# Adding the attention mask on VectorE instead of by a matmul, and normalising x2 ahead of it in VectorE's order

## The chip, the cores and the metric

The program runs on one core of a Trainium2 chip. The metric is the device time of one execution in microseconds (us). Five engines work on their own instruction streams and meet only at semaphores: TensorE (PE in the profile, PEld for its weight loads), VectorE (DVE), ScalarE (ACT), GpSimd (POOL) and SyncE (SP). ACT and SP also issue the transfers (ACTq, SPq in the trace are the sequencers of these engines).

## The reference

128 items (B), each a 128 x 512 float32 matrix `x` (128 positions, 512 features), pass through four residual stages. The ids of an item choose its mask, adapter and category weights.

```
# stage 0: attention with a mask that depends on the item's kind (0, 1 or 2)
scores = einsum(tanh(x @ W1 + b1), v)                       # one score per position
mask   = prefix (l <= j), postfix (l >= j) or cloze (l != j)
p      = softmax(where(mask, scores, -1e30))                # rows j, columns l
x      = x + (p @ x) / cnt
# stage 1: adapter of the item's language, then layer norm, gamma, beta
h      = relu(x @ w1[lang] + b1) @ w2[lang] + b2
x      = x + norm(x + h) * gamma[lang] + beta[lang]
# stage 2: x = x + zX * lap_x(x) + zY * lap_y(x) + zR * x * (1 - x)
# stage 3: x = x + x @ W[cat] + b[cat]
```

## The kernel before, in words

Everything is unrolled in Python. An item is one tile of 128 partitions. The work is a software pipeline in slots: slot `s` does the attention of item `s`, the adapter of item `s-1`, the normalisation of item `s-2`, the stencil of item `s-3`, the transpose of `x3` for item `s-4` and the category matmul of item `s-5`. There are 133 slots; the first five fill the pipeline and the last five drain it. Items are sorted by category, and the 1 MB category weights `w3s` are loaded only when the category is a new one (otherwise the transfer is skipped).

No scheduler is involved: the order of every engine is the order in which its `slot` function calls the helpers, and each helper waits for the semaphores of what it reads and overwrites. An instruction that waits holds up everything behind it on its engine.

The names that matter here, with their lines in the profile:

- `attn_tanh` (L553, ACT) makes `attn`; `attn_scores` (L371 and L372, PE) multiplies a matrix `v_wide`, whose columns are all `v`, with `attn`, which puts the same score row on all 128 partitions of `ps_scores`, and then accumulates the mask by a second matmul, bfloat16 identity times mask.
- `row_max` (L694, DVE) takes the negated maximum of each row of `ps_scores`; `exponentials` (L503, ACT) makes `probs` and their sum; `denominator` (L715) and `row_scale` (L721) on DVE and `scale_rows` (L527, ACT) make `mix`; `mix_transpose` (L388, PE) and `add_identity` (L727, DVE) make `mixT`.
- `pool` (L400), `adapter_hidden` (L393), `adapter_project` (L382) and `adapter_up` (L409) are the PE's part of attention and adapter; `variance` (L518, ACT), `add_epsilon` (L744), `center` (L735) and `normalize` (L759, DVE) give `x2`.
- `add_columns` (L772) and `add_rows` (L782) on DVE give `x3`, which `x3_transpose` (L417, PE) turns, `move_x3T` (L497, ACT) copies and `category` (L431, PE) multiplies with the category weights.
- `load_params` (L239) reads an item's ids from SBUF into registers of one engine. In the instruction stream it is a `TENSOR_LOAD`. ACT reads three values with one such instruction per item, right after `scale_rows` and ahead of the transfer of the next `xT` (L569) and of `attn_tanh`; SP reads four; DVE reads one (the language), between `add_adapted` (L701) and `mean` (L707).

On ACT a slot runs: read the ids, issue the `xT` load (L569), `attn_tanh`, `variance`, issue the `x` load, `relu`, `column_ends`, `exponentials`, `reaction` (L543), `move_x3T`, `move_xw` (L511), issue the `b3` load (L576), `scale_rows`.

Of the kernel before, what the change touches and what calls it, by code (L numbers as in the profile page):

```python
# [12 lines left out]
P = 128  # L13
# [51 lines left out]
def cond_residual_kernel(nc, x, xT, ids, cols, w1a,  # L65
# [22 lines left out]
    with ctx:  # L88
# [3 lines left out]
        v_wide = sb("v_wide", [P, P])  # L92
# [6 lines left out]
        ident16 = sb("ident16", [P, P], BF16)  # L99
# [39 lines left out]
        attn = sb("attn", [P, 2, S])  # L139
        neg_max = sb("neg_max", [P, 2])  # L140
# [37 lines left out]
        def out_bank(j):  # L178
# [27 lines left out]
        score_tables, item_tables = sem("score_tables"), sem("item_tables")  # L206
# [14 lines left out]
        max_ready, denom_ready, scale_ready, mix_ready, x1_b2_ready, x1_beta_ready = (  # L221
            sem(n) for n in ("max_ready", "denom_ready", "scale_ready", "mix_ready", "x1_b2_ready", "x1_beta_ready"))
# [77 lines left out]
        def _(pe):  # L300
# [63 lines left out]
            def attn_scores(b, kind):  # L364
                pe.wait_ge(attn_ready, b.upto())
                if b.is_first:
                    pe.wait_ge(score_tables, 1)
                    pe.wait_ge(gconst, 3)
                if b.is_at_least(1):
                    pe.wait_ge(mixT_ready, b.upto(1))  # L370
                pe.matmul(ps_scores, v_wide[:, :], attn[:, b.ring(2), :], start=True, stop=False)  # L371
                pe.matmul(ps_scores, ident16[:, :], masks16[:, bass.ds(kind * P, P)], start=False, stop=True  # L372
                          ).then_inc(scores_mm, 1)
# [64 lines left out]
            def slot(s):  # L438
                if s.inside(B):
                    words[(s).n] = load_params(pe, LANG, 2, s)  # L440
# [14 lines left out]
                if s.inside(B):  # L455
                    attn_scores(s, words[(s).n][1])
# [15 lines left out]
        def _(act):  # L472
# [26 lines left out]
            def exponentials(b):  # L499
# [3 lines left out]
                nc.scalar.activation(probs[:, b.ring(2), :], ps_scores, ACT.Exp,  # L503
# [121 lines left out]
        def _(dve):  # L625
# [46 lines left out]
            nc.vector.tensor_scalar(v_wide[:, :], ident[:, :], 0.0, vals[:, V:V + 1], ALU.mult, ALU.add)  # L672
            nc.vector.tensor_copy(ident16[:, :], ident[:, :]).then_inc(score_tables, 1)
# [14 lines left out]

            def row_max(b):
                p = b.ring(2)  # L690
                dve.wait_ge(scores_mm, b.upto())
                if b.is_at_least(2):
                    dve.wait_ge(probs_ready, b.upto(2))
                nc.vector.tensor_reduce(neg_max[:, p:p + 1], ps_scores, AX.X, ALU.max, negate=True  # L694
# [105 lines left out]
            def slot(s):  # L800
                if s.inside(B):
                    row_max(s)
                if (s - 2).inside(B):
                    normalize(s - 2)
# [160 lines left out]
```

## Time and profile before

| | |
|---|---|
| median of 3 runs | 1071.29 us (1068.22 to 1071.43) |
| profiled execution, its own time | 1066.62 us |
| its span | 1064.8 us |
| PE busy | 1046.7 us (98%) |
| DVE busy | 890.6 us (84%) |
| ACT busy | 501.5 us (47%) |
| POOL busy | 528.0 us (50%) |
| TensorE's granted clock | full in all 40 slices |
| mean of the transfers | 252 GB/s |

The span runs from the first to the last recorded instruction; the rest of the execution's own time lies around it. In the groups of instructions `L694 DVE ... x128 | 36.2, 283 | 3.1` is the line, the engine, the count, the busy time in us, the mean duration in ns, and the idle time of the engine just before these instructions, with what ended it. A float32 matmul appears as two MATMUL records (two passes); their ends are modelled, so the distance between two starts tells what a pass costs. In the timeline the first column is the start and the second the duration, both in us, and "xN" counts instructions merged into one row.

### The profile page before, as it was taken

Reading aid. Unit: us, or ns where it says so; the run is one execution under the profiler, and the core shown is the slowest. Engines: PE = TensorE matmul, PEld = TensorE weight load, DVE = VectorE, ACT = ScalarE, POOL = GpSimd, SP = SyncE. Lnnn points to the kernel's source line nnn. Section 1 sums busy time; section 2 is a strip of 40 time slices with the busy share of each in tenths; the row PEclk is TensorE's granted clock in tenths of the full one; section 3 lists DMA queues with packets and bytes.
Section 4 is the critical chain, followed back from the end, with each engine's and each line's share of the span. In section 5 each row is a group of like instructions: output and inputs, shape, how many; then the busy total and the mean of one; then the engine's idle time right before and its main releaser. Section 6 shows DMA issues by size and latency. Waiting matters only on the chain.

```text
span 1064.8 us, 22722 instructions
## 1 busy us (share of the span) xinstructions
PE 1046.7 (98%) x4912; PEld 653.1 (61%) x4912; DVE 890.6 (84%) x2090; ACT 501.5 (47%) x1422; POOL 528.0 (50%) x537
## 2 busy tenths in 40 slices
PE   5999999999999999999999999999999999999998
PEld 3666666666666666666666666666666666666663
DVE  5788888888888888888888888888888988888886
ACT  3544544444444445445445444444444444444442
POOL 3355455455445545545545544554544554554454
PEclk9999999999999999999999999999999999999999
DMA  8787897687878987766786778788788788887875
GB/s 334 228 271 225 265 303 238 211 259 246 263 244 279 322 250 243 242 220 211 241 255 213 247 225 269 250 289 266 228 271 269 245 250 266 276 283 233 274 221 175
DMA packets 119108, 268.82 MB, mean 252 GB/s; under 512 B 13010, under 2 KB 13028, under 8 KB 111556
## 3 DMA queue, kind: packets, MB, share of 16 engines
q1 hardware_dynamic: 63428, 166.24, 47.8%
q10 hardware_dynamic: 55552, 101.15, 31.3%
q8 instruction: 48, 0.79, 0.3%
q14 instruction: 80, 0.66, 0.2%
HBM read 243.21 MB, written 33.55 MB: 260 GB/s over the span
## 4 chain that ended last, share of the span: by engine, by line
PE 96%; DVE 1%; issue 1%; DMA 1%; POOL 1%; ACTq 0%; ACT 0%; POOLq 0%; DVEq 0%; SPq 0%
PE ps_out L431 40%; PE bank_hidden L382 11%; PE ps_attn L360 11%; PE ps_adapt L409 10%; PE ps_pool L400 10%; PE ps_x3T L417 5%; PE bank_scores L371 3%; PE bank_hidden L393 3%; PE bank_scores L388 1%; PE bank_scores L372 1%; DMA b_wide<-in_b 0%; DMA col_rows<-in_cols 0%; POOL b_wide L909 0%; DVE ps_adapt L701 0%; POOL rows_near L902 0%
## 5 line engine op out<-in xcount | busy, mean ns | idle before, releaser
L431 PE MATMUL ps_out<-w3s,x3T 128*128 x1016 | 498.3, 600 | 0.8 <-ACT x3T L497 0.8
L896 POOL TENSOR_TENSOR neighbours<-x 128x510 f32<-128x510 f32 x128 | 132.6, 1036 | 214.9 <-DVE x L759 214.9
L431 PEld LDWEIGHTS ps_out<-w3s,x3T 128*128 128x128 f32 x1016 | 164.1, 191 | 103.1 <-issue 101.5
L888 POOL TENSOR_TENSOR rstd<-var_eps,minus_half 128x1 f32<-128x1 f32 x128 | 70.2, 548 | 272.1 <-DVE var_eps L744 272.0
L902 POOL TENSOR_TENSOR rows_near<-rows_near 128x512 f32<-128x512 f32 x128 | 162.8, 1272 | 30.5 <-DMA rows_near<-x 30.3
L360 PEld LDWEIGHTS ps_attn<-xts,w_attn 128*128 128x128 f32 x1024 | 134.3, 191 | 61.2 <-issue 60.9
L909 POOL TENSOR_TENSOR b_wide<-b_wide,x 128x512 f32<-128x512 f32 x128 | 162.7, 1271 | 4.2 <-DMA b_wide<-in_b 4.2
L553 ACT ACTIVATE attn<-ps_attn,vals 128x128 f32<-128x128 f32 x128 | 47.0, 367 | 246.6 <-issue 160.2
L360 PE MATMUL ps_attn<-xts,w_attn 128*128 128x128 f32 x1024 | 135.1, 275 | 0.5 <-issue 0.5
L382 PE MATMUL bank_hidden<-w_all,xts 128*128 x1024 | 135.4, 275 | 0.0
L701 DVE SCALAR_TENSOR_TENSOR ps_adapt<-ps_adapt,x_b 128x512 f32<-128x512 f32 x128 | 89.1, 696 | 52.3 <-PE ps_adapt L409 51.3
L409 PE MATMUL ps_adapt<-w_all,hid 128*128 x256 | 131.3, 594 | 0.0
L400 PE MATMUL ps_pool<-xs,mixT 128*128 128x512 f32 x256 | 130.9, 593 | 0.0
L382 PEld LDWEIGHTS bank_hidden<-w_all,xts 128*128 128x128 f32 x1024 | 124.6, 192 | 1.8 <-issue 1.7
L417 PEld LDWEIGHTS ps_x3T<-ident,x 128*128 128x128 f32 x512 | 62.6, 141 | 71.9 <-issue 45.8
L543 ACT ACTIVATE ps_react<-x,c_t,nzr_t 128x512 f32<-128x512 f32 x128 | 99.0, 774 | 3.8 <-DVE x L782 3.8
L735 DVE SCALAR_TENSOR_TENSOR ps_adapt<-ps_adapt,neg_mean,gamma_wide 128x512 f32<-128x512 f32 x128 | 96.9, 757 | 2.2 <-issue 0.8
L782 DVE SCALAR_TENSOR_TENSOR x<-rows_near,wide_rows,ps_react 128x512 f32<-128x512 f32 x128 | 94.5, 738 | 1.5 <-POOL rows_near L902 1.4
L772 DVE SCALAR_TENSOR_TENSOR ps_react<-neighbours,wide_rows,ps_react 128x512 f32<-128x512 f32 x128 | 95.5, 746 | 0.1
L759 DVE SCALAR_TENSOR_TENSOR x<-ps_adapt,rstd,x_beta 128x512 f32<-128x512 f32 x128 | 94.8, 741 | 0.8 <-POOL rstd L888 0.8
L497 ACT ACTIVATE x3T<-ps_x3T 128x512 f32<-128x512 f32 x128 | 75.7, 592 | 40.6 <-PE ps_x3T L417 40.2
L534 ACT ACTIVATE hid<-bank_hidden,vals 128x128 f32<-128x128 f32 x128 | 47.0, 367 | 98.0 <-PE bank_hidden L393 96.5
(114 smaller groups left out, 1326.9 us busy)
## 6 DMA issues: line engine op xcount, KB each, us to landing
w3s<-in_w SPq DMA_DIRECT2D x128, 1024.0 KB
rows_near<-x SPq DMA_DIRECT2D x256, 252.0 KB
xts<-in_xT ACTq DMA_DIRECT2D x128, 256.0 KB, 4.4
xs<-in_x ACTq DMA_DIRECT2D x128, 256.0 KB, 4.7
b_wide<-in_b ACTq DMA_DIRECT2D x128, 256.0 KB, 4.6
out_x<-res SPq DMA_DIRECT2D x128, 256.0 KB, 4.4
w_all<-in_w1l SPq DMA_DIRECT2D x1, 2560.0 KB, 10.9
w_all<-in_w2l SPq DMA_DIRECT2D x1, 2560.0 KB, 16.6
```

The lines of the kernel that those rows point to most:

```text
L360: mm = pe.matmul(ps_attn, w1_attn[:, k * A:(k + 1) * A], xts[:, r, k, :], start=(k == 0), stop=(k == K - 1))
L382: mm = pe.matmul(ps_xw, xts[:, s.ring(3), k, :], w1_all[:, bass.ds(lang * (K * A) + k * A, A)], start=(k == 0), stop=(k == K - 1))
L400: pe.matmul(ps_pool[:, :], mixT[:, d.ring(2), :], xs[:, d.ring(2), :], start=True, stop=True).then_inc(pool_mm, 1)
L409: pe.matmul(ps_adapt[:, :], hid[:, g.ring(2), :], w2_all[:, bass.ds(lang * D, D)], start=True, stop=True).then_inc(adapt_mm, 1)
L417: mm = pe.transpose(ps_x3T[:, k * P:(k + 1) * P], x3[:, i.ring(2), k * P:(k + 1) * P], ident[:, :])
L431: mm = pe.matmul(out_bank(j)[:, :], x3T[:, j.ring(2), k * P:(k + 1) * P], w3s[:, bass.ds(wslot * (K * D) + k * D, D)], start=(k == 0), sto ...
L543: nc.scalar.activation(ps_react[:, :], x2[:, h.ring(2), :], ACT.Identity, bias=c0_t[:, bass.ds(h.n, 1)], scale=nzr_t[:, bass.ds(h.n, 1)]). ...
L735: nc.vector.scalar_tensor_tensor(normed[:, :], y[:, :], neg_mean[:, q:q + 1], gamma_wide[:, bass.ds(lang * D, D)], ALU.add, ALU.mult).then ...
L772: nc.vector.scalar_tensor_tensor(ps_react[:, :], neighbours[:, q, :], zx_t[:, bass.ds(i.n, 1)], ps_react[:, :], ALU.mult, ALU.add).then_in ...
L896: nc.gpsimd.tensor_tensor(neighbours[:, q, 1:D - 1], x2[:, q, 0:D - 2], x2[:, q, 2:D], ALU.add).then_inc(neighbours_ready, 1)
L902: nc.gpsimd.tensor_tensor(above[:, q, :], above[:, q, :], below[:, q, :], ALU.add).then_inc(rows_ready, 1)
L909: nc.gpsimd.tensor_tensor(b3_wide[:, q, :], b3_wide[:, q, :], x3[:, q, :], ALU.add).then_inc(x3_b3_ready, 1)
```

## The change

The mask no longer goes through TensorE. `attn_scores` is one matmul whose weights are the column `v` broadcast over 128 columns (no `v_wide`, no `ident16`), and TensorE reads one id per item instead of two. A new VectorE helper `add_mask` adds the bfloat16 mask to `ps_scores` on the way out of PSUM into a new SBUF tile `masked`; `row_max` and `exponentials` read `masked`. VectorE therefore reads two ids per item (language and kind), one slot ahead. In VectorE's slot `normalize(s - 2)` now stands first, and `add_mask(s)` and `row_max(s)` behind it; before, `row_max(s)` stood first.

```diff
-            def attn_scores(b, kind):
+            def attn_scores(b):
                 pe.wait_ge(attn_ready, b.upto())
-                if b.is_first:
-                    pe.wait_ge(score_tables, 1)
-                    pe.wait_ge(gconst, 3)
                 if b.is_at_least(1):
                     pe.wait_ge(mixT_ready, b.upto(1))
-                pe.matmul(ps_scores, v_wide[:, :], attn[:, b.ring(2), :], start=True, stop=False)
-                pe.matmul(ps_scores, ident16[:, :], masks16[:, bass.ds(kind * P, P)], start=False, stop=True
-                          ).then_inc(scores_mm, 1)
+                pe.matmul(ps_scores, vals[:, V:V + 1].broadcast_to([A, P]), attn[:, b.ring(2), :],
+                          start=True, stop=True).then_inc(scores_mm, 1)
...
-                nc.scalar.activation(probs[:, b.ring(2), :], ps_scores, ACT.Exp,
+                nc.scalar.activation(probs[:, b.ring(2), :], masked[:, :], ACT.Exp,
...
+            def add_mask(b, kind):
+                dve.wait_ge(scores_mm, b.upto())
+                if b.is_first:
+                    dve.wait_ge(gconst, 3)
+                if b.is_at_least(1):
+                    dve.wait_ge(probs_ready, b.upto(1))
+                nc.vector.tensor_tensor(masked[:, :], ps_scores, masks16[:, bass.ds(kind * P, P)], ALU.add
+                                        ).then_inc(masked_ready, 1)
+
             def row_max(b):
                 p = b.ring(2)
-                dve.wait_ge(scores_mm, b.upto())
-                if b.is_at_least(2):
-                    dve.wait_ge(probs_ready, b.upto(2))
-                nc.vector.tensor_reduce(neg_max[:, p:p + 1], ps_scores, AX.X, ALU.max, negate=True
+                dve.wait_ge(masked_ready, b.upto())
+                nc.vector.tensor_reduce(neg_max[:, p:p + 1], masked[:, :], AX.X, ALU.max, negate=True
                                         ).then_inc(max_ready, 1)
...
             def slot(s):
-                if s.inside(B):
-                    row_max(s)
                 if (s - 2).inside(B):
                     normalize(s - 2)
+                if s.is_first:
+                    words[s.n] = load_params(dve, LANG, 2, s)
+                if s.inside(B):
+                    add_mask(s, words[s.n][1])
+                    row_max(s)
...
-                if s.inside(B):
-                    words[(s).n] = load_params(dve, LANG, 1, s)
+                if (s + 1).inside(B):
+                    words[(s + 1).n] = load_params(dve, LANG, 2, s + 1)
```

On DVE, the part of a slot of the full pipeline that follows `center`, before the change (L782 is `x3`, L694 the row maximum, L759 `x2`, L752 the result, L715 the denominator):

```order
L735 SCALAR_TENSOR_TENSOR ps_adapt<-ps_adapt,neg_mean,gamma_wide 128x512
L782 SCALAR_TENSOR_TENSOR x<-rows_near,wide_rows,ps_react 128x512 [waits x3T_mm,x3_b3_ready,rows_ready,columns_ready]
L694 TENSOR_REDUCE neg_max<-bank_scores 128x1 [waits probs_ready,scores_mm]
L759 SCALAR_TENSOR_TENSOR x<-ps_adapt,rstd,x_beta 128x512 [waits rstd_ready,norm_ready]
L752 TENSOR_TENSOR res<-ps_out,b_wide 128x512 [waits res_out1,x3_b3_ready,out_mm]
L715 TENSOR_SCALAR denom<-prob_sum,count_t 128x1 [waits probs_ready]
```

The same part after the change (L688 is the mask addition):

```order
L735 SCALAR_TENSOR_TENSOR ps_adapt<-ps_adapt,neg_mean,gamma_wide 128x512
L782 SCALAR_TENSOR_TENSOR x<-rows_near,wide_rows,ps_react 128x512 [waits x3T_mm,x3_b3_ready,rows_ready,columns_ready]
L759 SCALAR_TENSOR_TENSOR x<-ps_adapt,rstd,x_beta 128x512 [waits rstd_ready,norm_ready]
L688 ISA [waits probs_ready,scores_mm]
L688 TENSOR_TENSOR masked<-bank_scores,masks 128x128
L694 TENSOR_REDUCE neg_max<-masked 128x1 [waits masked_ready]
L752 TENSOR_TENSOR res<-ps_out,b_wide 128x512 [waits res_out0,x3_b3_ready,out_mm]
L715 TENSOR_SCALAR denom<-prob_sum,count_t 128x1 [waits probs_ready]
```

Between `x3` and the row maximum now stand `x2` and the mask addition; the result and the denominator follow as before.

On PE, the part of a slot around the scores, before the change (L388 turns `mix`, L393 is `adapter_hidden`, L400 `pool`):

```order
L388 MATMUL bank_scores<-ident,mix 128x128 [waits mix_ready]
L393 MATMUL bank_hidden<-mixT,xw 128x128 [waits mixT_ready,xw_ready]
L371 MATMUL bank_scores<-attn,v_wide 128x128 [waits mixT_ready,attn_ready]
L372 ISA
L372 MATMUL bank_scores<-masks,ident 128x128
L400 MATMUL ps_pool<-xs,mixT 128x512 [waits x1_beta_ready,x_in1]
```

The same part after the change:

```order
L383 MATMUL bank_scores<-ident,mix 128x128 [waits mix_ready]
L388 MATMUL bank_hidden<-mixT,xw 128x128 [waits mixT_ready,xw_ready]
L367 MATMUL bank_scores<-attn,vals 128x128 [waits mixT_ready,attn_ready]
L395 MATMUL ps_pool<-xs,mixT 128x512 [waits x1_beta_ready,x_in1]
```

One matmul and the register instruction ahead of it are gone, and the weights of the other one come from `vals`.

## Rows read from the trace of the kernel before

**Rows 1.** The page: busy time, share of the span and instructions; the chain that ended last.

```profile
PE 1046.7 (98%) x4912; PEld 653.1 (61%) x4912; DVE 890.6 (84%) x2090; ACT 501.5 (47%) x1422; POOL 528.0 (50%) x537
...
PE 96%; DVE 1%; issue 1%; DMA 1%; POOL 1%; ACTq 0%; ACT 0%; POOLq 0%; DVEq 0%; SPq 0%
```

**Rows 2.** Timeline of PE: the scores matmul of slots 6 and 127.

```profile
58.90 0.39 PE L371 MATMUL bank_scores<-attn,v_wide 128*128 128x128 f32 x2
...
1033.19 0.39 PE L371 MATMUL bank_scores<-attn,v_wide 128*128 128x128 f32 x2
```

**Rows 3.** Timeline of PE from the scores of slot 61 to the transpose of x3.

```profile
501.96 0.39 PE L371 MATMUL bank_scores<-attn,v_wide 128*128 128x128 f32 x2
...
502.19 0.22 PE L372 MATMUL bank_scores<-masks,ident 128*128 x1
...
502.24 1.08 PE L431 MATMUL ps_out<-w3s,x3T 128*128 x2
...
503.16 1.02 PE L400 MATMUL ps_pool<-xs,mixT 128*128 128x512 f32 x2
...
504.02 0.60 PE L417 MATMUL ps_x3T<-ident,x 128*128 128x128 f32 x4
```

**Rows 4.** Groups by line and shape: weight loads, the identity addition, the tanh.

```profile
L372 PEld LDWEIGHTS bank_scores<-masks,ident 128*128 128x128 bf16 x128 | 12.8, 100 | 0.0
...
L312 PEld LDWEIGHTS ps_pool<-lang_parts,pick 96*128 96x128 bf16 x5 | 0.5, 98 | 2.1 <-DVE beta_wide L686 2.1
...
L727 DVE TENSOR_TENSOR mixT<-bank_scores,ident 128x128 f32<-128x128 f32 x128 | 37.2, 290 | 25.1 <-PE bank_scores L388 23.3
...
L553 ACT ACTIVATE attn<-ps_attn,vals 128x128 f32<-128x128 f32 x128 | 47.0, 367 | 246.6 <-issue 160.2
```

**Rows 5.** Timeline of DVE in slot 50: x3, row maximum, x2, result.

```profile
414.69 0.74 DVE L782 SCALAR_TENSOR_TENSOR x<-rows_near,wide_rows,ps_react 128x512 f32<-128x512 f32 x1
415.34 0.29 DVE L694 TENSOR_REDUCE neg_max<-bank_scores 128x1 f32<-128x128 f32 x1
415.55 0.74 DVE L759 SCALAR_TENSOR_TENSOR x<-ps_adapt,rstd,x_beta 128x512 f32<-128x512 f32 x1
416.20 0.68 DVE L752 TENSOR_TENSOR res<-ps_out,b_wide 128x512 f32<-128x512 f32 x1
```

**Rows 6.** Timeline of PE in slot 50: the transpose of x3.

```profile
415.49 0.66 PE L417 MATMUL ps_x3T<-ident,x 128*128 128x128 f32 x4
```

**Rows 7.** Timeline of ACT and its sequencer, from the tanh of slot 50 to the next.

```profile
412.79 0.37 ACT L553 ACTIVATE attn<-ps_attn,vals 128x128 f32<-128x128 f32 x1 [2.94 <-issue]
...
415.67 0.37 ACT L503 ACTIVATE probs<-bank_scores,neg_max 128x128 f32<-128x128 f32 x1 [1.49 <-DVE neg_max L694]
...
417.71 0.40 ACT L527 ACTIVATE mix<-probs,scale 128x128 f32<-128x128 f32 x1 [0.23 <-DVE scale L721]
419.89 0.36 ACTq L569 DMA_DIRECT2D xts<-in_xT  x1
420.35 0.37 ACT L553 ACTIVATE attn<-ps_attn,vals 128x128 f32<-128x128 f32 x1 [2.24 <-issue]
```

**Rows 8.** Line 239 on ACT, then on DVE: duration ns min/median/max, first and last start.

```profile
L239 ACTq TENSOR_LOAD <-all_params x128: 705/1445/2673, 14.6 to 1013.3; - x128
...
L239 DVEq TENSOR_LOAD <-all_params x128: 307/696/1395, 25.2 to 1037.7; - x128
```

**Rows 9.** Timeline of slots 61 and 62: scaling, next xT issue, category weights.

```profile
506.14 0.40 ACT L527 ACTIVATE mix<-probs,scale 128x128 f32<-128x128 f32 x1 [0.32 <-issue]
...
507.71 0.34 ACTq L569 DMA_DIRECT2D xts<-in_xT  x1
...
512.11 0.36 SPq L263 DMA_DIRECT2D w3s<-in_w  x1
...
514.19 0.40 ACT L527 ACTIVATE mix<-probs,scale 128x128 f32<-128x128 f32 x1 [0.32 <-issue]
...
516.50 0.36 ACTq L569 DMA_DIRECT2D xts<-in_xT  x1
```

More of the change, by code:

```diff
@@ L91, in cond_residual_kernel @@
         w1_attn = sb("w1_attn", [P, K * A])
-        v_wide = sb("v_wide", [P, P])
         w1_all = sb("w1_all", [P, L * K * A])
@@ L98, in cond_residual_kernel @@
         ident = sb("ident", [P, P])
-        ident16 = sb("ident16", [P, P], BF16)
         masks16 = sb("masks16", [P, 3 * P], BF16)
@@ L139, in cond_residual_kernel @@
         attn = sb("attn", [P, 2, S])
+        masked = sb("masked", [P, S])
         neg_max = sb("neg_max", [P, 2])
@@ L205, in cond_residual_kernel @@
             sem(n) for n in ("b2_spread", "beta_spread", "b2_moved", "beta_moved"))
-        score_tables, item_tables = sem("score_tables"), sem("item_tables")
+        item_tables = sem("item_tables")
         params_made = sem("params_made")
@@ L219, in cond_residual_kernel @@
         edges_ready = sem("edges_ready")
-        max_ready, denom_ready, scale_ready, mix_ready, x1_b2_ready, x1_beta_ready = (
-            sem(n) for n in ("max_ready", "denom_ready", "scale_ready", "mix_ready", "x1_b2_ready", "x1_beta_ready"))
+        masked_ready, max_ready, denom_ready, scale_ready, mix_ready, x1_b2_ready, x1_beta_ready = (
+            sem(n) for n in ("masked_ready", "max_ready", "denom_ready", "scale_ready", "mix_ready", "x1_b2_ready", "x1_beta_ready"))
         y_ready, mean_ready, vareps_ready, norm_ready, x2_ready = (
@@ L439, in slot @@
                 if s.inside(B):
-                    words[(s).n] = load_params(pe, LANG, 2, s)
+                    words[(s).n] = load_params(pe, LANG, 1, s)
                     attn_project(s)
@@ L455, in slot @@
                 if s.inside(B):
-                    attn_scores(s, words[(s).n][1])
+                    attn_scores(s)
                 if (s - 5).inside(B):
@@ L671, in _ @@
             ins.then_inc(wide_made, 1)
-            nc.vector.tensor_scalar(v_wide[:, :], ident[:, :], 0.0, vals[:, V:V + 1], ALU.mult, ALU.add)
-            nc.vector.tensor_copy(ident16[:, :], ident[:, :]).then_inc(score_tables, 1)
             dve.wait_ge(sorted_made, 1)
```

## The prediction

> **What bounds the kernel now.** I read the page first, then PE's timeline, then the timelines of DVE and ACT in slots where they run late, and last the reads of ids into registers. The page says that PE is busy for 98% of the span and is 96% of the chain that ended last [rows 1]. The scores matmul starts at 58.90 in slot 6 and at 1033.19 in slot 127 [rows 2]: 121 slots in 974.29 us, 8.052 us each. So nearly everything depends on the length of a slot, and that of PE's instructions is what sets it, with next to no waiting.
>
> But a second chain runs beside PE, and it closes on itself once per slot. In slot 50 the tanh starts at 412.79 and the row maximum at 415.34 (2.55 later: variance on ACT, epsilon, center and x3 on DVE lie between and are all in a row), the exponentials at 415.67 (0.33), the scaling of the rows at 417.71 (2.04: reaction, the copies of x3T and xw), the next xT issue at 419.89 (2.18) and the next tanh at 420.35 (0.46) [rows 5, 7]. The reader should see in these rows that no link waits for PE: this is a ring through ACT, DVE and ACT again, of 5.38 us plus X, where X is the time from the scaling to the xT issue. X is the read of three ids into registers: 705 ns at best, 1445 at the median, 2673 at worst [rows 8], plus some 0.2 around it. X is 1.57 in slot 61, where no category weights are moving, and 2.31 in slot 62, in which they were issued 2.08 before the scaling [rows 9]. Its mean follows from the tanh group: 246.6 us idle ahead of 128 tanh is 1.93 each, and since the scaling takes 0.40 and the issue-to-tanh step is 0.46, X is about 1.93 + 0.40 - 0.46 = 1.87 [rows 4, 7]. The ring thus takes 7.25 on average against PE's 8.04. It has 0.8 to spare and only touches PE in single slots: in slot 50, x3 ends at 415.43 and PE's transpose starts at 415.49 right behind it [rows 5, 6], 0.06 late.
>
> **What the change removes from PE.** Seen from its start, the mask matmul lasts 0.05 until the next one (502.19 to 502.24). I don't trust that: from 501.96 to 503.16 there are two float32 passes over 128 columns, the mask, and two passes over 512 columns, 1.20 in all; two 512-column passes cost 0.86 (503.16 to 504.02), two 128-column ones 0.23 (501.96 to 502.19) [rows 3]. The mask therefore costs 0.11, the 0.10 of a weight load [rows 4] that the short bfloat16 pass doesn't cover for the matmul behind it. PE's own slot falls to 7.93.
>
> The Trainium skill (TensorE: Matmul & The Clock Gate, section Back-to-back issue gap) gives an isolated warm matmul of N columns N/2.4 + 2.5 ns, 56 ns here; by that PE would get back 0.056 a slot, half of what the rows say, and the same page warns that it leaves the weight load out. The rows decide.
>
> The weights of the scores now come from a broadcast column. The nearest rows: a broadcast bfloat16 load 98 ns, a plain one 100 [rows 4]; I take nothing. If a float32 one were slower, its cover is the pass before it, and what stands out would be at most another 0.10 a slot, eating the gain. The second id that PE no longer reads and the register instruction cost nothing now, since PE's sequencer runs ahead of it. The two set-up instructions removed on DVE lie ahead of a wait for PE and save nothing.
>
> **What it adds to the ring.** The row maximum stood 0.65 behind x3. Now x2 stands there (0.65 from its start to the next one, 415.55 to 416.20), then the mask addition, then the maximum [rows 5]. The addition is a 128x128 read of PSUM and SBUF like the identity addition, 0.29 [rows 4]; the maximum must wait for its result, so nothing overlaps, and I add 0.04 for the semaphore. From x3 to the row maximum that is 0.65 + 0.65 + 0.33 instead of 0.65: 0.98 more. It is the largest term of the change, and no part of it is covered in a slot where the ring is late, because x3, x2, the mask and the maximum are consecutive on one engine and ACT waits for the maximum. The exponentials read SBUF now instead of PSUM: no row separates the two, between -0.03 and +0.03, taken as 0. From the exponentials to the scaling I take 1.93 instead of 2.04: the scaling in slot 50 waited for the reciprocal on DVE [rows 7], and that comes earlier behind the exponentials now, since x2 no longer stands between. The ring is 5.38 + 0.98 - 0.11 = 6.25 plus X.
>
> X itself: DVE now reads two ids, at the same time as ACT reads three. The bounds for what this does to X are 0 and one register's share, (705 - 307)/2 = 0.20 [rows 8]. Against that, the ring is later behind the issue of the category weights, so that less of their transfer is left when the ids are read; at best every X would be 1.57. X thus lies between 1.57 and 2.07, and I take 1.85. The ring is then 8.10.
>
> **The sum.** The ring at 8.10 is above PE's 7.93, so PE waits at the transpose of x3; queued behind that on PE are the adapter's projections, adapter_up and the next item's attention, and DVE and ACT wait for those. The slot goes from 8.05 to 8.10: 121 x 0.05 = +6 us, where PE alone would have given 121 x -0.12 = -14. Slow and quick X alternate, and a slot cannot be shorter than 7.93, so some of the quick ones are wasted; I add 0.01 a slot, +1. In the five slots of filling, PE has waits anyway and the longer chain counts between 0 and 0.98 a slot, 0 to +5; I take +2. In the drain the ring is gone after the last item, and DVE enters it up to 1 later; +1. Total +10: the profiled execution's 1066.6 becomes 1077, and the median of the runs, 4.7 above it, becomes 1071.3 + 10 = 1081.
>
> DVE's own load is no bound: 890.6 us busy and 128 x 0.33 = 42 more is 933 of some 1075 [rows 1]. A slower mean, because two ids are read ahead of it, comes 0.2 to 0.4 later; the variance waits for the tanh later than that.
>
> **The rivals.**
> 1. PE stays the bound. If X falls towards 1.57 because the category weights are out of the way, the ring is 7.82 and every slot 7.93 to 7.97: -14 to -10, plus 3 for fill and drain, 1061 to 1065. For it: slot 61 shows that X without that traffic is 1.57, and with the items sorted by category many slots load none. Against it: the mean of 1.87 is what 128 slots gave, and it would have to fall by 0.2. This is the case that is not slower, and it decides at a mean X of 7.93 - 6.25 = 1.68.
> 2. The ring is as long as PE's slot was. With X near 1.77 the slot is 8.02 to 8.04, fill and drain add 3, and the time is 1068 to 1074, no difference that can be measured.
> 3. The ring is worse than I say: no shortening behind the exponentials (+0.11), and X at 1.87 plus part of the register's share. The slot is 8.25 to 8.35, +24 to +36, plus 4: 1099 to 1111. For it: the mean X as it stands, with 2.04 and 0.98, already gives 8.23. Against it: the reciprocal does come earlier.
> 4. The change doesn't take the mask's 0.11 off PE, since the broadcast weights load slower or since the next weight load was never exposed. It would only move rival 1 to between 1066 and 1071 and leaves the forecast, which the ring sets, where it is.
>
> **How the numbers follow.** The forecast (ring binds, slot 8.05 to 8.20, 1074.5 to 1093) has 0.42, rival 3 0.17, rival 2 0.16 and rival 1 with the faster part of rival 4 0.25. A measurement of this kernel can tell 0.3%, 3.2 us, from no change. Slower by more than that is the forecast and rival 3, with a little of it lost at the border: 0.58; within it 0.17; faster 0.25. The time predicted is the forecast's, 1081. The range takes in most of rival 1 and the lower part of rival 3: 1062 to 1100; for the forecast alone it is 1074 to 1093.
>
> **What would show it.** The pass over the mask is gone and the two starts around it, scores to pool, are 1.09 apart instead of 1.20. Row maximum behind x3 by 1.63 instead of 0.65. The tanh of a typical slot starts less than 1 us ahead of the scores matmul, and PE shows waits for x3 at its transpose in most slots, not in a few. Slots of 8.0 to 8.2 with the ones that load weights the longest. The ring's account is wrong if PE still shows no waits and all slots are 7.93, and the size of X is wrong if the mean idle time ahead of the tanh is not between 1.5 and 2.1.

## The result and the profile after

The changed kernel takes 1066.20 us (median of 20 runs, 1062.28 to 1071.08), the kernel before 1069.58 in the same comparison (20 runs, 1068.11 to 1075.32). The ratio is 0.9965 with a 95% interval of 0.9952 to 0.9978: faster by 0.35%, little but clear of zero. The forecast was 1081, slower. The profiled executions lie closer together than the medians: 1065.58 after, with a span of 1063.7, against 1066.62. A trace shows one execution, and those of the changed kernel are spread over 9 us: counts of slots from two traces that differ by a few say little.

The page after, answering to [rows 1]: busy time per engine, then the chain that ended last.

```profile
PE 1040.2 (98%) x4784; PEld 639.1 (60%) x4784; DVE 918.9 (86%) x2216; ACT 480.7 (45%) x1422; POOL 528.2 (50%) x537
...
PE 40%; issue 32%; POOL 21%; DVE 2%; POOLq 0%; ACTq 0%; DVEq 0%; ACT 0%
```

PE has 128 instructions fewer and is 6.5 us less busy. And the chain has moved: it was PE for 96%, now PE is 40%, and the rest is put down to POOL (21%) and to "issue" (32%). That is not the ring of ACT and DVE: traced back, the chain stays on POOL there, through waits for which it names no cause. So this line says that PE is no longer all of it, and the timelines have to say what the rest is. That PE's share fell and the kernel did not get slower is the first thing to explain.

PE's timeline, answering to [rows 2, 3]: the scores matmul of slots 6 and 127, and in slot 59 from the scores over the pool matmul to the transpose of x3.

```profile
61.77 0.39 PE L367 MATMUL bank_scores<-attn,vals 128*128 128x128 f32 x2
...
489.17 0.39 PE L367 MATMUL bank_scores<-attn,vals 128*128 128x128 f32 x2
...
490.25 1.02 PE L395 MATMUL ps_pool<-xs,mixT 128*128 128x512 f32 x2
491.11 0.60 PE L412 MATMUL ps_x3T<-ident,x 128*128 128x128 f32 x4
...
1032.23 0.28 PE L367 MATMUL bank_scores<-attn,vals 128*128 128x128 f32 x1
```

The 121 slots take 970.46 us now against 974.29 [rows 2]. From scores to pool it is 1.08 instead of 1.20 [rows 3]. Taken slot by slot from the same matmul, a slot of the kernel before is nearly always 8.04 us: 7 slots are longer by over 0.03 and the excess of all is 1.1 us. In the changed kernel 91 slots are within 0.03 of 7.93, and 30 are longer, with 10.4 us over it in all. So the profiled execution sums up as: fill +2.9 (slot 6 begins at 61.77, not at 58.90), PE's own slots 121 x -0.109 = -13.2, long slots 10.4 - 1.1 = +9.3, drain -0.1: together about -1.0, which is what the two executions differ by.

Timeline of DVE in slot 59, answering to [rows 5]: x3, x2, mask, row maximum. Behind it the groups of the mask's addition, the exponentials and the tanh, by line, answering to [rows 4].

```profile
489.35 0.74 DVE L782 SCALAR_TENSOR_TENSOR x<-rows_near,wide_rows,ps_react 128x512 f32<-128x512 f32 x1
490.01 0.75 DVE L759 SCALAR_TENSOR_TENSOR x<-ps_adapt,rstd,x_beta 128x512 f32<-128x512 f32 x1
490.67 0.28 DVE L688 TENSOR_TENSOR masked<-bank_scores,masks 128x128 f32<-128x128 f32 x1
490.99 0.29 DVE L694 TENSOR_REDUCE neg_max<-masked 128x1 f32<-128x128 f32 x1
```

```profile
L688 DVE TENSOR_TENSOR masked<-bank_scores,masks 128x128 f32<-128x128 f32 x128 | 35.8, 280 | 3.0 <-PE bank_scores L367 3.0
...
L498 ACT ACTIVATE probs<-masked,neg_max 128x128 f32<-128x128 f32 x128 | 51.5, 402 | 216.0 <-DVE neg_max L694 215.9
...
L548 ACT ACTIVATE attn<-ps_attn,vals 128x128 f32<-128x128 f32 x128 | 47.0, 367 | 230.6 <-issue 159.5 <-PE ps_attn L359 71.1
```

The row maximum stands 1.64 behind x3, as forecast. The tanh group has 230.6 us of idle ahead of it, 1.80 each; by the forecast's own working X is 1.80 + 0.40 - 0.46 = 1.74, and counted over the 120 slots of the full pipeline that another xT issue follows it is 1.79 on the mean (forecast 1.85; before the change, counted in the same way, 1.93).

Now the ring, in the slot before. The timeline of ACT with its sequencer, and of SP for its first line: category weights issued, scaling, xT issue, tanh, and a turn later exponentials, scaling, xT issue and tanh (answers to [rows 7, 9]).

```profile
474.82 0.36 SPq L262 DMA_DIRECT2D w3s<-in_w  x1
```

```profile
477.26 0.40 ACT L522 ACTIVATE mix<-probs,scale 128x128 f32<-128x128 f32 x1 [0.21 <-issue]
479.97 0.34 ACTq L564 DMA_DIRECT2D xts<-in_xT  x1
480.42 0.37 ACT L548 ACTIVATE attn<-ps_attn,vals 128x128 f32<-128x128 f32 x1 [2.76 <-issue]
...
484.28 0.40 ACT L498 ACTIVATE probs<-masked,neg_max 128x128 f32<-128x128 f32 x1 [2.38 <-DVE neg_max L694]
...
485.00 0.34 ACTq L571 DMA_DIRECT2D b_wide<-in_b  x1
...
486.02 0.39 ACT L522 ACTIVATE mix<-probs,scale 128x128 f32<-128x128 f32 x1
487.01 0.34 ACTq L564 DMA_DIRECT2D xts<-in_xT  x1
487.45 0.37 ACT L548 ACTIVATE attn<-ps_attn,vals 128x128 f32<-128x128 f32 x1 [1.04 <-issue]
```

Timeline of PE at the scores matmul and of PEld at the transpose of x3 in the slot that the tanh at 480.42 leads to, and behind them the wait of that line over the whole run (us, times, longest), after and then before.

```profile
481.12 0.39 PE L367 MATMUL bank_scores<-attn,vals 128*128 128x128 f32 x2
...
483.11 0.42 PEld L412 LDWEIGHTS ps_x3T<-ident,x 128*128 128x128 f32 x4 [0.72 <-DVE x L782]
```

```profile
PEld ps_x3T L412 <- DVE x L782: 37.4, 56, 1.8
```

```profile
PEld ps_x3T L417 <- DVE x L782: 25.3, 53, 1.3
```

With weights issued 2.44 us ahead of the scaling, X is 2.71; the tanh comes 0.70 ahead of the scores matmul of its slot and not 1.8, x3 comes late, and PE's weight loads wait for it. Such a wait is not yet a long slot: the kernel before has 53 of them and 7 long slots. One turn later, with no weights moving, X is 0.99 and the lateness is made good. And from the exponentials at 484.28 to the scaling it is 1.74, not 1.93.

Counted over the same 121 slots, from the same starts: 53 slots have a weights transfer issued in the 4.5 us ahead of their scaling (an issue of 0.36 us; one that is skipped takes 0.11), 68 have none. X has two values, not one (the last slot with weights has no next xT issue, so that 52 count for its mean):

| slots | X before | X after | long slots after | excess, us |
|---|---|---|---|---|
| 68 without weights | 1.70 | 1.35 | 0 | 0.0 |
| 53 with weights | 2.23 | 2.36 | 30 | 10.4 |

The links of the ring without X are 0.45, 1.90, 1.63, 0.32 and 1.74: 6.04. The ring is 7.39 in the first class, well below PE's 7.93, and 8.40 in the second. (The expectation of experiment 12 has 2.31 for 2.36, since it counts the slot without a next xT issue as nothing.) All 30 long slots are of the second class, as the 7 of the kernel before were. But 53 x 0.47 would be 25 us, and the excess is 10.4: in slots that are not long the tanh starts 1.77 us ahead of the scores matmul (the median), in the long ones 0.42 to 0.90. A late turn first uses up that lead, and quick turns restore it.

### The profile page after: what moved, and what is told of

It reads as the page before. It is cut to its first block, busy times and chain, and to the rows that moved or that the text cites. A ratio compares the mean times of both kernels' runs of the same rounds, so it can differ in the third digit from the quotient of the medians.

```text
span 1063.7 us, 22593 instructions
## 1 busy us (share of the span) xinstructions
PE 1040.2 (98%) x4784; PEld 639.1 (60%) x4784; DVE 918.9 (86%) x2216; ACT 480.7 (45%) x1422; POOL 528.2 (50%) x537
## 4 chain that ended last, share of the span: by engine, by line
PE 40%; issue 32%; POOL 21%; DVE 2%; POOLq 0%; ACTq 0%; DVEq 0%; ACT 0%
PE ps_out L426 17%; POOL b_wide L912 8%; POOL rows_near L905 8%; PE bank_hidden L377 5%; PE ps_attn L359 4%; PE ps_adapt L404 4%; PE ps_pool L395 4%; POOL rstd L891 4%; PE ps_x3T L412 2%; POOL neighbours L899 2%; DVE x L759 1%; PE bank_hidden L388 1%; PE bank_scores L367 1%; PE bank_scores L383 1%; DVE x L782 1%
## 5 line engine op out<-in xcount | busy, mean ns | idle before, releaser
L426 PE MATMUL ps_out<-w3s,x3T 128*128 x1016 | 491.7, 593 | 0.8 <-ACT x3T L492 0.8
L426 PEld LDWEIGHTS ps_out<-w3s,x3T 128*128 128x128 f32 x1016 | 164.1, 191 | 101.6 <-issue 101.5
L548 ACT ACTIVATE attn<-ps_attn,vals 128x128 f32<-128x128 f32 x128 | 47.0, 367 | 230.6 <-issue 159.5
L498 ACT ACTIVATE probs<-masked,neg_max 128x128 f32<-128x128 f32 x128 | 51.5, 402 | 216.0 <-DVE neg_max L694 215.9
L759 DVE SCALAR_TENSOR_TENSOR x<-ps_adapt,rstd,x_beta 128x512 f32<-128x512 f32 x128 | 95.4, 745 | 1.1 <-POOL rstd L891 1.0
L782 DVE SCALAR_TENSOR_TENSOR x<-rows_near,wide_rows,ps_react 128x512 f32<-128x512 f32 x128 | 94.5, 738 | 1.5 <-POOL rows_near L905 1.4
L765 DVE TENSOR_TENSOR ps_react<-ps_react,x 128x512 f32<-128x512 f32 x128 | 88.2, 689 | 0.9 <-ACT ps_react L538 0.9
## 6 DMA issues: line engine op xcount, KB each, us to landing
w_all<-in_w1l SPq DMA_DIRECT2D x1, 2560.0 KB, 10.4
```

The lines of the kernel that those rows point to most:

```text
L426: mm = pe.matmul(out_bank(j)[:, :], x3T[:, j.ring(2), k * P:(k + 1) * P], w3s[:, bass.ds(wslot * (K * D) + k * D, D)], start=(k == 0), sto ...
L759: nc.vector.scalar_tensor_tensor(x2[:, q, :], normed[:, :], rstd[:, q:q + 1], x1_beta[:, q, :], ALU.mult, ALU.add).then_inc(x2_ready, 1)
L782: nc.vector.scalar_tensor_tensor(x3[:, q, :], above[:, q, :], zy_t[:, bass.ds(i.n, 1)], ps_react[:, :], ALU.mult, ALU.add).then_inc(x3_rea ...
```

## The experiments

Four questions: what the order and the addition cost alone, whether the ring decides the long slots, what makes X long, and which version is best. Each run was timed against the kernel before on the same chip; I give the ratio to that. X and slots are counted from each trace as above, X without the last slot.

**1. The mask's move alone, x2 behind the row maximum.** The changed kernel with

```diff
-                if (s - 2).inside(B):
-                    normalize(s - 2)
                 if s.is_first:
                     words[s.n] = load_params(dve, LANG, 2, s)
                 if s.inside(B):
                     add_mask(s, words[s.n][1])
                     row_max(s)
+                if (s - 2).inside(B):
+                    normalize(s - 2)
```

> The changed kernel with one thing put back: VectorE does the mask addition and the row maximum first and x2 behind them, as the order was before. Theory R (a slot lasts as long as the longer of PE's stream, 7.94 us, and the ring tanh, x3, x2, mask, row maximum, exponentials, scaling, ids, tanh): x2's 0.66 leaves the ring, which falls from 6.06 + X to 5.40 + X, about 7.2 with the mean X of 1.80. The 30 of 121 slots above 7.94 should shrink to a few, slot mean 7.94 to 7.96, and filling gets about 2 us shorter: 9 to 12 us under the changed kernel, 1054 to 1057. Rival P (PE alone sets the slot, and the long slots come from transfers or from PE's own issue): the same 1066 as the changed kernel, with about 30 long slots. Rival V (VectorE's total load counts): 1066 too, since its work is the same.

1069.07 us, ratio 0.9987 (0.9972 to 1.0002). The forecast was missed by over 12 us. Slot 6 begins at 58.88, so the 2.9 us of fill belong to x2 in front; but there are 45 long slots, with 14 us over 7.93. From x3 to the row maximum it is 0.97, 0.66 less. But from the exponentials to the scaling it is 2.05 in late slots and no longer 1.74, because the reciprocal now comes behind x2 (the scaling's waits for it are the last two rows below). So the fixed links are 5.69, only 0.35 shorter. X took the rest back in slots without weights: 1.94 instead of 1.35, with 18 long slots among them; with weights it is 2.27. Line 238 on ACT and the wait at the transpose in this kernel (duration ns min/median/max, first and last start; us, times, longest), then the scaling's wait for the reciprocal in this kernel and in the changed one:

```profile
L238 ACTq TENSOR_LOAD <-all_params x128: 702/1930/3099, 14.2 to 1013.2; - x128
```

```profile
PEld ps_x3T L412 <- DVE x L782: 49.5, 89, 1.2
```

```profile
ACT mix L522 <- DVE scale L721: 27.4, 94, 0.8
```

```profile
ACT mix L522 <- DVE scale L721: 1.1, 2, 0.8
```

The median read is 1930 ns, where the changed kernel has 1374. X is no constant that a ring can be built from: it depends on where in the slot it falls.

**2. The order alone.** The kernel before with normalize(s - 2) ahead of row_max(s), mask on PE.

> The kernel before with only the order changed: x2 ahead of the row maximum, mask still by matmul. Theory R: the ring grows by 0.66 less what the reciprocal gives back, to about 5.75 + X, 7.6 on average against PE's 8.04. More slots than the 7 of before touch it, but few: slot mean 8.055 to 8.09, 0 to +5 us, and filling up to +3: 1070 to 1077. Rival P: 1069.6, no change. If x2 first were a gain of its own (x2 and its transfers start 0.2 us earlier), it would be faster than 1069.6.

1074.53 us, ratio 1.0036 (1.0021 to 1.0050). Fill +2.3, and 28 long slots. From x3 to the row maximum it is 0.66 more, from the exponentials to the scaling 1.70 and not 2.04, so that the ring is 0.32 longer. x2 ahead of the maximum costs by itself; it is no gain that the mask's move hides.

**3. The mask left out.** The kernel before without the second matmul of the scores; start=True, stop=True on the first.

> The kernel before without the mask matmul and without any mask in its place: the mask is left out of the computation, the rest is as before. It prices PE's part alone. Theory R with 0.11 us for the mask matmul: slots of 7.94, ring 5.38 + X well below, so 121 x 0.11 = 13 us less, 1055 to 1058. Rival: the mask matmul is worth its own 0.05 as the distance of the starts says, 6 to 7 us less, 1062 to 1064, with slots of 7.99.

1061.98 us, ratio 0.9908 (0.9891 to 0.9926). The number is the rival's, but not its reason: the common slot is 7.93, so that the pass does cost PE its 0.11 (0.109). In the traced execution, the slowest of six at 1065.22, there are 44 long slots with 12.9 us in all, 38 of them with weights, and X is 2.64 in the slots with weights. Even without any addition on DVE, a quicker PE runs into the ring.

**4. A second addition.** The changed kernel with one more of the same additions, into a tile that nobody reads, ahead of the real one.

> The changed kernel with the mask addition done twice: the first into a spare tile that nobody reads, the second as before. It adds 0.21 to 0.28 us to the ring and nothing to PE. Theory R: ring 6.30 + X, about 8.1 on average, above PE's 7.94: well over half of the slots go long, slot mean 8.10 to 8.20, 10 to 22 us over the changed kernel, 1076 to 1088. Rival P: 1066. Rival V: VectorE rises from 86% to 89% busy, still idle at times: 1066 to 1067.

1079.58 us, ratio 1.0079 (1.0064 to 1.0095), within theory R's range. x3 to row maximum is 1.83, 0.20 more. 55 slots are long instead of 30 (theory R had well over half of the 121), 46 of them with weights, with 22.1 us in all: 11.7 more than in the changed kernel, and the fill takes another 3.4. 0.20 in each of 55 slots is 11.0, so the ring decides in about half of the slots, and there nearly in full.

**5. The ids read and the xT issue out of the ring.** ACT waits 1.7 us on the mean for the row maximum; from the second item on they now stand in that wait.

```diff
-                if (s + 1).inside(B):
+                if (s + 1).inside(B) and s.n < 1:
                     words[(s + 1).n] = load_params(act, CAT, 3, s + 1)
                     load_xT(s + 1, words[(s + 1).n][1])
...
                     column_ends(s - 4)
+                if (s + 1).inside(B) and s.n >= 1:
+                    words[(s + 1).n] = load_params(act, CAT, 3, s + 1)
+                    load_xT(s + 1, words[(s + 1).n][1])
                 if (s - 1).inside(B):
                     exponentials(s - 1)
```

> The changed kernel with one move: ScalarE reads the next item's three ids and issues its xT load in its wait ahead of the exponentials, not behind the scaling of the mix, so X is no part of the ring of VectorE and ScalarE. Theory R (the ring decides the 30 long slots): the ring is then 6.0 to 6.3 us, far below the tensor engine's 7.94, so the long slots' 9.7 us go but for those that weights or first items cause: 1055 to 1060 us, PE above 98%. Rival F (the long slots come from somewhere else, from the four neighbour rows and the DMA queues): 1063 to 1067 us, the count of long slots near 30 as in the changed kernel. Rival C (the ids read then stands in the wait and is itself slow, 1.4 to 2.9 us, so that it pushes the exponentials): over 1068 us, row maximum to exponentials longer than 0.4.

1056.79 us, ratio 0.9884 (0.9863 to 0.9905), as the ring has it. Seven slots are long, with 2.0 us. The chain, the wait at the transpose, and the read in this kernel:

```profile
PE 90%; issue 3%; DVE 2%; POOL 1%; DVEq 0%; ACT 0%; ACTq 0%; POOLq 0%
```

```profile
PEld ps_x3T L412 <- DVE x L785: 11.2, 29, 1.2
```

```profile
L238 ACTq TENSOR_LOAD <-all_params x128: 692/707/1335, 14.6 to 1008.2; - x128
```

PE is the chain again. What I had not foreseen is that the read itself is 707 ns at the median there, as fast as it ever is.

**6. SyncE reads its ids ahead of the neighbour rows.** load_params(sp, FRESH, 4, s) ahead of shift_rows(s).

> The changed kernel with one move: SyncE reads its four ids ahead of the three neighbour-row copies, so that its read no longer starts about when ScalarE's does. Theory S (X is long when ScalarE's ids read meets SyncE's read): X falls to 1.0 to 1.3 us in most slots, from a mean of 1.80, long slots fewer than 30, 1058 to 1063 us. Rival T (X is long because of the copies and loads on the DMA queues, not of the other engine's read): X stays 1.6 to 1.9 on the mean, 1064 to 1068 us. Rival U (SyncE's read, now ahead of the copies, delays them, and x3 and the reaction come late): 1068 us or more, with the tensor engine waiting for x3.

1067.89 us, ratio 0.9981 (0.9962 to 0.9999). X is 1.64 on the mean instead of 1.79, long slots are 24 with 10 us. ACT's read still has 1386 ns at the median, and in 120 of 121 slots SP's read is over by then. SyncE's read beside it is not what makes it long: theory S falls. The move is not without effect, though: X is 1.77 in the slots with weights instead of 2.36, and 1.54 in the others instead of 1.35. It also puts the rows' copies nearer to ACT's read.

**7. Without the category's weights.** SyncE loads them for the first two items only.

> The changed kernel without the category's weights after the first two items (all later items are computed with the first two items' weights): the 1 MB-class loads of SyncE are gone, everything else stands. Theory T (X is long because of the traffic of the weights): X falls from a mean of 1.80 to 1.0 to 1.3, 1056 to 1062 us. Theory S (X is long because of the other engines' reads): X 1.6 to 1.8 and 1063 to 1067 us.

1056.14 us, ratio 0.9876 (0.9853 to 0.9899). No slot is over 7.94. The ids read and the wait:

```profile
L238 ACTq TENSOR_LOAD <-all_params x128: 698/730/1967, 13.6 to 1006.6; - x128
```

```profile
PEld ps_x3T L412 <- DVE x L783: 5.2, 5, 1.8
```

X is 1.08. It is 1.09 in the slots that had no weights in the changed kernel either, where it was 1.35. One thing goes with it: without the weights SyncE issues the neighbour rows earlier, 2.77 us ahead of ACT's read at the median, where it was 2.23 in the changed kernel's slots without weights and 1.99 in those with. So the run does not tell the weights themselves from the place of the rows.

**8. VectorE reads its ids once.** It starts its own read 0.27 us behind ScalarE's in nearly every slot, so it was a suspect as well.

> The changed kernel with VectorE reading its two ids for the first item only (all later items take the first item's mask and language in VectorE's additions). Theory V (ScalarE's ids read is long because VectorE's starts 0.27 us behind it): X falls by 0.5 to 0.8 in the slots without weights and by 0.5 or more in those with, long slots under 15, 1056 to 1061 us. Theory Q (it is long because of the neighbour rows and the weights on the DMA queues and SyncE's read): X falls by under 0.3, 1062 to 1067 us, the long slots still those with weights.

1065.11 us, ratio 0.9947 (0.9928 to 0.9966). X is 1.34 and 2.39, long slots 31, all with weights.

```profile
L238 ACTq TENSOR_LOAD <-all_params x128: 697/1346/2820, 13.5 to 1011.2; - x128
```

ACT's read is what it was (1374 at the median): theory Q, not V.

**9. VectorE reads two ids in the kernel before.** The count in load_params(dve, LANG, ...) is 2 instead of 1.

> The kernel before with VectorE reading two ids instead of one (the second is not used). Theory R: VectorE's read grows by 0.2 us, the ring's X by 0.0 to 0.2, which the kernel before has room for: 1068 to 1071 us. Rival H (a longer read of VectorE slows the other engines' reads by as much as it is longer, 0.4 on the mean): X over 2.2, long slots 25 or more, 1072 to 1077 us.

1070.59 us, ratio 1.0010 (0.9993 to 1.0026), no difference. X is 1.93 on the mean in both. The second id costs nothing that the times can show; the one trace has 21 long slots with 3.3 us, against 7 with 1.1.

**10. The ids read out of the ring, in the kernel before.** The edit of experiment 5.

> The kernel before with one move: ScalarE reads the three ids and issues the xT load in its wait ahead of the exponentials; the mask stays on the tensor engine and x2 behind the row maximum. Theory R (ring and tensor engine by slot): the kernel before had 7 long slots with 1.45 us in all over its floor of 8.04, so that taking X out of its ring can give back 1 to 3 us at the most: 1065 to 1069 us; the 12 to 13 us that the move gave beside the mask's move are then the 0.105 us a slot of the mask matmul, which only the move lets through. Rival G (the ids read itself is worth its time everywhere, also where the tensor engine bounds): 1056 to 1062 us.

1066.09 us, ratio 0.9969 (0.9953 to 0.9985). Every slot is 8.04, none is long. Out of the ring the read is worth 0.3% where PE's slot is 8.04, and 9 to 12 us where it is 7.93 (experiments 5 and 11, against the changed kernel and experiment 1).

**11. Mask moved, x2 behind, ids in the wait.** Experiments 1 and 5 together.

> Both moves: the mask's addition by VectorE, x2 back behind the row maximum, and ScalarE's ids read and xT load in the wait ahead of the exponentials. Theory R: the ring is 5.4 us, the floor of the tensor engine 7.94 in nearly every slot, and the fill that putting x2 first cost is back (2.9 us): 1052 to 1057 us, 2 to 4 us below the kernel with the ids read in the wait and x2 first. Rival F (x2 behind the row maximum delays the neighbour rows, and the tensor engine waits at the transposes of x3): 1060 to 1068 us, long slots 20 or more.

1055.44 us, ratio 0.9874 (0.9851 to 0.9896): the lowest median of all kernels here (its interval overlaps that of experiment 5), 14 us below the kernel before in the same comparison, and by the two ratios 0.9% below the changed kernel. Ten slots are long, with 2.5 us; the fill is back (slot 6 begins at 59.07). ACT's wait is shorter here than the read and the issue in it: the exponentials start 0.92 behind the row maximum and not 0.32, which the ring has room for.

```profile
PE 94%; issue 2%; DVE 2%; POOL 1%; DMA 1%; DVEq 0%; ACT 0%; ACTq 0%; POOLq 0%; SPq 0%
```

**12. Weights issued behind the neighbour rows.** If weights ahead of the read are the trouble, they could go a little later.

```diff
                     shift_rows(s)
+                if (s - 1).inside(B):
+                    load_w3(s - 1, ...)
+                if s.inside(B):
                     words[(s).n] = load_params(sp, FRESH, 4, s)
...
-                if s.inside(B):
-                    load_w3(s, ...)
```

> The changed kernel with one move in SyncE's order: an item's category weights are issued behind the next item's three neighbour-row copies, not ahead of them, so that the weights no longer enter the queues 2.45 us before ScalarE's ids read. Theory W (in the changed kernel all 30 long slots are among the 53 with weights, where X is 2.31 on the mean against 1.35 without, because the weights lie ahead of the rows and of the read): X falls below 1.9 in nearly every slot, long slots under 10, 1056 to 1060 us. Rival N (the weights only move, and now lie under the read itself, or come late for the tensor engine): X 2.2 or more in the slots with weights, or a wait of the tensor engine for the weights, 1064 to 1072 us.

1073.15 us, ratio 1.0025 (1.0006 to 1.0044). Both were half right, and the time is above both ranges. X fell to 1.21 in the slots whose items bring weights and 1.24 in the others, and the wait for x3 nearly went. But PE now waits for the weights. ACT's read; then the waits of PEld for x3 and ahead of the category's weight loads (101.5 us in the changed kernel); then the worst place on PE's timeline:

```profile
L238 ACTq TENSOR_LOAD <-all_params x128: 700/884/2243, 14.4 to 1021.6; - x128
```

```profile
PEld ps_out L427 <- issue: 117.3, 413, 2.9
...
PEld ps_x3T L413 <- DVE x L783: 4.3, 7, 1.7
```

```profile
237.06 1.05 PE L360 MATMUL ps_attn<-xts,w_attn 128*128 128x128 f32 x8
240.27 1.46 PE L427 MATMUL ps_out<-w3s,x3T 128*128 x2 [2.16 <-issue]
```

The profile calls that wait "issue", since the landing of the weights has no instruction to be put down to; that it is the weights I infer from the edit and from the line. The 24 long slots have 15.8 us over 7.93. PE itself idles for 10.4 us in 12 such waits; part of the rest is the lower clock behind the longest of them (last section). The place of the weights is a trade between ACT's read and PE's own need.

## Why the prediction was wrong

**What bounds the kernel** was read rightly: PE, and beside it a ring of ACT and DVE that touches it in single slots. Experiments 4 and 5 show both: 0.20 more in the ring made nearly twice as many long slots, and cutting it made every slot but seven PE's own.

**The removal from PE** was right in size: 0.109 a slot in the changed kernel and in experiment 3, forecast 0.11. The Trainium skill (TensorE: Matmul & The Clock Gate, section Back-to-back issue gap) would have given 0.056 for an isolated pass of 128 columns, and about 0.081 in a stream of weight loads and matmuls; the measurement is above both and decides. The broadcast column costs nothing: 192 ns a load before (`v_wide`) and after (`vals`). Rival 4 falls.

**The addition to the ring** was right: x3 to row maximum 1.63 to 1.64 against 1.63 forecast, the mask's addition 280 ns against 290.

**The exponentials** I took at no cost for reading SBUF. They went from 368 to 402 ns, 0.03 more, the upper end of my bounds. The Trainium skill (Perfetto Trace Analysis, section Optimizing Scalar/DVE Operations) has an overhead of about 93 ns for ScalarE on SBUF and about 51 ns on PSUM, 42 ns apart; the trace has 34, the same way and near it.

**From the exponentials to the scaling** is the first step that failed: "From the exponentials to the scaling I take 1.93 instead of 2.04". It is 1.74 in slots that are late, in slot 58 too. I had let the reciprocal come earlier, but not followed ACT's queue behind that: with nothing to wait for it is 1.10 to the x3T copy, 0.48 to xw and 0.16 to the scaling, and the b3 issue at 485.00 runs under the reaction. The order of x2 is what does it: with the mask on PE, x2 first brings this link from 2.04 to 1.70 (experiment 2), and with x2 put back it is 2.05 (experiment 1). So x2 first adds 0.66 to the ring and takes 0.3 away, where I had taken away 0.11. The ring is 6.04 + X, not 6.25 + X, and by my own threshold, 7.93 less the ring, PE stays the bound up to a mean X of 1.89 and not 1.68. X is 1.79. That alone moves the case from the forecast to rival 1.

**X** is the second step. Its mean was forecast well (1.85, measured 1.79), partly by luck: I had it fall because less of the weights' transfer would be left, and in the slots with weights it rose, from 2.23 to 2.36, while it fell in those without, from 1.70 to 1.35. And "The ring is then 8.10" put it into every slot. X has two values, which [rows 9] showed in two neighbouring slots and which I noted in the reading and then averaged away. 68 slots are at 7.93 whatever the ring does below that, and the 53 with weights pay only what is above it, less the lead that the slots between give back. How much each step is worth can be estimated from the trace: I carry the tanh's lead from slot to slot with the measured X; a scaling is never earlier than 4.07 behind the scores matmul (slot 57), PE is late when the lead is under 0.81 (slot 58: 0.70, and 0.11 over 7.93), and a scores matmul never starts less than 0.42 behind its tanh. With links of 6.04 that gives 29 long slots and 10 us, as measured; with the forecast's 6.25 it gives 17 us, and with 6.04 and X at its mean in every slot none. The forecast had 121 x 0.17 = 21 us over PE's floor. So of the 10 us too many some 7 are the first step and 3 the mean; and once the links are right, the mean would hide the 10 us that are there. That and the fill were to be set against 13.

**The fill** cost 2.9, forecast 2, within its bounds of 0 to 5; it comes from x2 ahead of the maximum (2.3 with that alone in experiment 2, nothing without it in 1 and 11). The drain cost nothing, forecast 1.

**Rival 1**, PE stays the bound, is nearest with 1061 to 1065; the median is 1.2 above it. It too is not quite what happened, since it had "every slot 7.93 to 7.97", and its reason, the weights out of the way for X, did not come true. As a change it had -11 to -7 with fill and drain, and the medians moved by -3.4, so that the result lies between rivals 1 and 2. The stated range, 1062 to 1100, holds it only because it was stretched over rival 1. I had also counted from a median of three runs, 1071.3, which is 1069.6 with twenty. The observations that I had named came out so: scores to pool 1.08, right; row maximum 1.63, right; idle ahead of the tanh 1.80, right; waits for x3 "in most slots", wrong (56 waits, 30 long slots of 121); the tanh less than 1 us ahead of the scores "in a typical slot", wrong (1.8 in those, 0.4 to 0.9 in the long ones); the slots with weights the longest, right.

**The expected 13 us** therefore went into long slots (9.3) and fill (2.9) of the profiled execution. Experiment 11 gets them: 14 us in the medians, once the ids read leaves the ring and x2 goes back (3 to 4 of which the move of the read gives without the change, experiment 10).

**What stays open** is why the read of three registers takes from 0.70 to 2.9 us. It is not VectorE's or SyncE's read (experiments 6, 8 and 9), and it is short without weights (7), with weights later (12), and at another place in the slot with the weights as they are (5). Why X is 1.94 without weights in experiment 1, when the neighbour rows are issued 0.84 us nearer to the read, isn't explained by the weights. That the rows' own copies take part fits: the first of them is issued 2.8 us ahead of the read in experiments 7 and 12, 2.2 in the changed kernel, 1.8 in experiment 3 and 1.4 in experiment 1, and X without weights is 1.1 to 1.2, 1.35, 1.82 and 1.94. It is not shown, since no run here takes them away, and the kernel before (2.2 and 1.70) and experiment 6 (1.7 and 1.54) don't lie on that line.

## What to carry to other kernels

A ring beside the bounding engine counts slot by slot: carry its lateness from slot to slot. A mean of the ring against a mean of the engine gives no long slot here, the longer of the two in each class gives 25 us, and 10 were measured. Most of a gain of 0.11 a slot on PE was lost to a chain that, once changed, had 0.1 to spare on the mean and none in 53 slots of 121. And an instruction moved within one engine's order has two prices, what it delays and what it lets through earlier: here 0.66 and 0.3. Before an instruction is taken off the bound, look for what stands in the second chain without need: a read of ids and a DMA issue that could lie in a wait of the same engine were worth 9 to 12 us once PE was quicker, against 3.4 for the change, and 3 to 4 without it. And a link of such a chain whose durations are spread as those of the read here (705, 1445, 2673 ns) can depend on its place; try it elsewhere before sizing anything else.

## What was not expected of the hardware

- A read of ids into registers on ACT took 707 ns (three ids) at the median when it stood ahead of the exponentials, and 1374 behind the scaling, with the same transfers per slot. The shortest reads are 307 ns for one id (VectorE before), 522 for two (VectorE after) and 698 for three, some 200 ns more for each; the Trainium skill (Runtime: NRT & Kernel Launch, section Instruction fetch mechanics) has about 200 ns a register, and the trace agrees for the fastest; the page speaks of registers loaded from HBM, and these reads are from SBUF. Behind the scaling the same read takes up to 2881 ns.
- Leaving one matmul out of every slot moved the kernel by 0.9% with 0.109 us of 8.04 (1.4%) removed. X rose with it, from 2.23 to 2.64 in the slots with weights. That a faster PE shifts the other engines' reads against the transfers fits this, and is not shown.
- The wait of 2.16 us on PE in experiment 12 was followed by a granted clock of 0.50, its lower level of 1.2 GHz, for 3.4 us (from 240.9). Busy time of PE in the microsecond that follows, then the clock, the DMA share and GB/s:

```profile
241.00:242.00 1.00, 1.00 (x3) 0.50 1.04 379
```

  The changed kernel, whose weight load waits 0.72 in slot 58 while matmuls still run, kept 2.4 GHz there.
